# Turning the combined expert rows: TensorE transposes against a pass through HBM and VectorE's block transpose, in a fused attention and mixture-of-experts kernel

## What is computed

```python
x = hidden_states                       # (2, 1024, 512)
xn = layernorm(x)
# attention, one head of width 512, no mask
q, k, v = split(xn @ w_qkv.T + b_qkv)
s = softmax(q @ k.T / sqrt(512)) @ v @ w_out.T + b_out
# experts
logits = xn @ router_w + router_b
w = softmax(top2(logits))               # two weights for each token
h_e = silu(xn @ expert_w[e] + expert_b[e])
combined = sum over the two chosen e of w_e * h_e
y = xn + combined @ proj_w + proj_b
g = silu(norm_w * y / rms(y))
out = x + s * g
```

## Time and profile before

| | us |
|---|---|
| median of 3 runs | 490.43 (489.11 to 491.26) |
| the profiled execution | 490.71 |
| its span, first to last instruction | 489.0 |
| TensorE busy | 478.2 (98%) |
| VectorE busy | 312.5 (64%) |
| ScalarE busy | 207.7 (42%) |
| GpSimd busy | 205.4 (42%) |

### The profile page before, as it was taken

The page is one execution under the profiler, slowest core; times in us unless marked ns, Lnnn a source line. Parts: engine busy times, 40 slices in busy tenths (PEclk is TensorE's granted clock), DMA queues, the critical chain, the costliest instruction groups (busy, mean ns, idle before and its releaser), DMA issues.

```text
span 489.0 us, 7145 instructions
## 1 busy us (share of the span) xinstructions
PE 478.2 (98%) x2146; PEld 388.1 (79%) x2147; DVE 312.5 (64%) x474; ACT 207.7 (42%) x300; POOL 205.4 (42%) x289
## 2 busy tenths in 40 slices
PE   6999999999999999999999999999999999999995
PEld 3688787888888888878888888878888878888884
DVE  2657152578632436979888888762597754857762
ACT  1265463143331154736444444322655441644550
POOL 2145210005887859703000000744568873377234
PEclk9999999999999999999999999999999999999999
DMA  8764999966888599897996666897555864445512
GB/s 309 272 238 166 379 382 369 390 207 227 294 294 304 188 334 304 252 295 205 262 282 202 195 200 184 310 305 267 158 156 170 264 192 147 138 158 170 172 47 84
DMA packets 77630, 115.77 MB, mean 237 GB/s; under 512 B 6608, under 2 KB 36320, under 8 KB 77600
## 3 DMA queue, kind: packets, MB, share of 16 engines
q1 hardware_dynamic: 63872, 77.62, 50.4%
q0 software_dynamic: 7440, 25.45, 14.7%
q10 hardware_dynamic: 6288, 12.33, 7.1%
HBM read 66.09 MB, written 49.28 MB: 236 GB/s over the span
## 4 chain that ended last, share of the span: by engine, by line
PE 92%; DVE 3%; DMA 2%; issue 2%; SPq 0%; ACT 0%; DVEq 0%
PE ab L1589 20%; PE ab L1590 20%; PE ab L1591 20%; PE sc L1589 7%; PE sc L1591 7%; PE sc L1590 7%; PE sc L1605 3%; PE tp L1595 2%; DMA xg<-rows_scratch 2%; PE tp L1639 2%; DVE y L1468 1%; PE sc L1668 1%; DMA raw_v<-in_w_qkv 1%; PE ab L1613 1%; PE sc L1671 1%
## 5 line engine op out<-in xcount | busy, mean ns | idle before, releaser
L781 POOL DMA_INDIRECT y<-y_scratch,pos x32 | 33.3, 1042 | 88.8 <-DMA y_scratch<-yt_so 74.2
L1589 PE MATMUL ab<-W,st_h 128*128 x156 | 60.8, 390 | 0.6 <-DVE st_l L1297 0.6
L1591 PE MATMUL ab<-W,st_l 128*128 x156 | 60.7, 389 | 0.0
L1590 PE MATMUL ab<-W,st_h 128*128 x156 | 60.7, 389 | 0.0
L764 POOL DMA_INDIRECT rows_scratch<-xb,pos x32 | 31.2, 974 | 51.0 <-DVEq L1285 42.8
L1589 PE MATMUL sc<-xt_h,t_h 128*128 128x512 f32 x128 | 50.1, 391 | 0.0
L1591 PE MATMUL sc<-xt_h,t_l 128*128 128x512 f32 x128 | 49.8, 389 | 0.0
L1590 PE MATMUL sc<-xt_l,t_h 128*128 128x512 f32 x128 | 49.8, 389 | 0.0
L1026 ACT CAST st_h<-tp 128x512 fp32r<-128x512 f32 x39 | 22.9, 587 | 41.1 <-PE ab L1591 39.0
L1353 DVE TENSOR_REDUCE small<-sc 128x1 f32<-128x1024 f32 x16 | 19.5, 1222 | 24.3 <-PE sc L1591 21.9
L1589 PEld LDWEIGHTS ab<-W,st_h 128*128 128x128 f32 x156 | 29.3, 188 | 7.1 <-issue 1.0
(11 more groups left out here) (270 smaller groups left out, 1197.2 us busy)
## 6 DMA issues: line engine op xcount, KB each, us to landing
rows_scratch<-xn ACTq DMA_DIRECT2D x3, 3328.0 KB, 20.2
xb<-in_expert_w POOLq DMA_DIRECT2D x6, 1024.0 KB
xn<-rows_scratch SPq DMA_DIRECT2D x48, 128.0 KB, 3.4
xg<-rows_scratch SPq DMA_DIRECT2D x44, 128.0 KB
y_scratch<-yt_own SPq DMA_DIRECT2D x20, 256.0 KB, 3.1
y_scratch<-yt_so SPq DMA_DIRECT2D x19, 256.0 KB, 2.9
p_scratch<-prob SPq DMA_DIRECT2D x9, 512.0 KB, 2.9
rows_scratch<-xs SPq DMA_DIRECT2D x16, 256.0 KB, 5.9
```

The lines of the kernel that those rows point to most:

```text
L781: pool.indirect_dma_start(y[:, q, :], None, y_d, bass.IndirectOffsetOnAxis(pos[:, GB * s + p:GB * s + p + 1], 0))\
L1589: nc.tensor.matmul(dst, lh, rh, start=start, stop=False)
L1590: nc.tensor.matmul(dst, lh, rl, start=False, stop=False)
L1591: return nc.tensor.matmul(dst, ll, rh, start=False, stop=stop)
```

## The change

The eight transposes of `turn_comb` are gone from TensorE. The combined rows now take the way of the probabilities. `add_bias` writes the expert's rows with the columns in the order (a c q), so that gathered and combined rows have that order already. `pass_combined(p)` on SP waits for `combine(p)`, stores the two tiles of `y1` in HBM (`c_scratch`, 512 KB), waits for the landing, and loads them into the place of the pair's `y2` rows with four DMAs of 128 KB. `c_turn(p)` on VectorE waits for these (`comb_in`), transposes the 32x32 blocks into `tp` in two instructions, and counts `p1_turned`. `c_split` and GpSimd's `gather_pair` now wait for `p1_turned` where they waited for TensorE's `tp_full`. The tables OUT and TURN number the uses of `p1_out` and `p1_turned`, which combined rows and probabilities now share.

Three orders change with it. On VectorE `c_turn(j+3)` stands between `weigh(j+2)` and `row_max(j+2)`. On ScalarE `exp(j+2)` stands ahead of `c_split(j+3)`. On SP `pass_combined(0)` stands in the middle of the stage's first loads, 1 and 2 stand ahead of `pass_on(0)`, and the later ones behind `pass_on`, `store_1` and `load_x1` of their turn. The semaphore `bc_done` is merged into `pre`.

```diff
+    c_d = nc.dram_tensor("c_scratch", (GB, 2, P, D), F32).ap()
+    c_v = c_d.rearrange("p t s h -> p s t h")
+    c_q = c_d.rearrange("p t (r s) (a f) -> p a s t r f", r=4, a=4)
...
+            def pass_combined(p):
+
+                q = 2 * (p % 2)
+                sp.wait_ge(c_done, 2 * p + 2)
+                sp.dma_start(c_v[p], y1[:, q:q + 2, :]).then_inc(p1_out, 16)
+                sp.wait_ge(p1_out, 16 * OUT["c", p])
+                for a in range(4):
+                    sp.dma_start(y2[32 * a:32 * (a + 1), q:q + 2, :].rearrange("p t (r f) -> p (t r) f", r=4),
+                                 c_q[p, a, :, :, :, :].rearrange("s t r f -> s (t r) f")).then_inc(comb_in, 16)
+
+            pass_combined(0)
             sp.wait_ge(ab_full, U["v", 1, GB - 1] + 1)
...
-            pool.wait_ge(tp_full, 1)
+            pool.wait_ge(p1_turned, TURN["c", 0])
             gather_pair(2)
...
             def c_split(p):
-                act.wait_ge(tp_full, p + 1)
+                act.wait_ge(p1_turned, TURN["c", p])
                 nc.scalar.copy(st_h[:, :, :, :], tp[:, :, :, :]).then_inc(tp_hi, 1)
...
-                if j + 3 < GB:
-                    c_split(j + 3)
                 if j == GB - 3:
                     p_split(GB - 2)
                 if j + 2 < GB:
                     exp(j + 2)
+                if j + 3 < GB:
+                    c_split(j + 3)
...
-                vec.tensor_tensor(yt[h], ab[:, (U["e", 0] + h) % 2, :],
-                                  bias_e[:, ds(e, 1), :].rearrange("p a n -> p (a n)"), ALU.add).then_inc(ab_read, 1)
+
+                vec.tensor_tensor(yt[h].rearrange("p (a c q) -> p c a q", a=4, q=32),
+                                  ab[:, (U["e", 0] + h) % 2, :].rearrange("p (c a q) -> p c a q", a=4, q=32),
+                                  bias_e[:, ds(e, 1), :].rearrange("p o (c a q) -> p (o c) a q", a=4, q=32),
+                                  ALU.add).then_inc(ab_read, 1)
...
+            def c_turn(p):
+                q = 2 * (p % 2)
+                dve.wait_ge(comb_in, 64 * (p + 1))
+                if p == 0:
+                    dve.wait_ge(g_lo, ROWS)
+                else:
+                    dve.wait_ge(tp_lo, TU["c", p])
+                for s in range(2):
+                    last = vec.transpose(tp[:, s, :, :].rearrange("p c (r s) -> p c r s", r=4),
+                                         y2[:, q + s, :].rearrange("p (r c q) -> p c r q", r=4, q=32))
+                last.then_inc(p1_turned, 1)
...
             combine(1)
+            c_turn(0)
             c_low(0)
...
             add_product(0, 1)
+            c_turn(1)
             c_low(1)
             combine(2)
             weigh(0)
             row_max(GB)
             add_product(1, 0)
             add_product(1, 1)
+            c_turn(2)
             c_low(2)
...
                 if j + 2 < GB:
                     weigh(j + 2)
+                if j + 3 < GB:
+                    c_turn(j + 3)
+                if j + 2 < GB:
                     row_max(GB + j + 2)
...
-            def turn_comb(p):
-                pe.wait_ge(c_done, 2 * p + 2)
-                if p == 0:
-                    pe.wait_ge(g_lo, ROWS)
-                else:
-                    pe.wait_ge(tp_lo, TU["c", p])
-                q = 2 * (p % 2)
-                transpose_tile(y1[:, q, :], 0)
-                transpose_tile(y1[:, q + 1, :], 1).then_inc(tp_full, 1)
```

More of the change, by code:

```diff
@@ L109, in gated_attention_moe @@
         TU[k] = len(TU)
+    OUT, TURN = {}, {}
+    for k in ([("c", 0), ("c", 1), ("c", 2), ("t", 0)]
+              + [u for p in range(GB - 2) for u in [("t", p + 1)] + ([("c", p + 3)] if p + 3 < GB else [])]):
+        OUT[k] = len(OUT) + 1
+    for k in ([("c", 0), ("c", 1), ("c", 2), ("t", 0)]
+              + [u for j in range(GB - 2) for u in ([("c", j + 3)] if j + 3 < GB else []) + [("t", j + 1)]]):
+        TURN[k] = len(TURN) + 1
     with ExitStack() as ctx:
@@ L278, in gated_attention_moe @@
         q_hi = sem("q_hi")
-        bc_done = sem("bc_done")
         const = sem("const")
@@ L351, in gated_attention_moe @@
         p1_in = sem("p1_in")
+        comb_in = sem("comb_in")
         p1_turned = sem("p1_turned")
@@ L678, in pass_on @@
                                  p_q[j, a, :, :, :]).then_inc(p1_in, 16)
+            pass_combined(1)
+            pass_combined(2)
             pass_on(0)
@@ L693, in _ @@
                         load_x1(p + 1)
+                if p + 3 < GB:
+                    pass_combined(p + 3)
                 if p + 4 < GB:
@@ L1615, in bias_products @@
             def bias_products():
-                pe.wait_ge(bc_done, 1)
                 for m, (high, low) in enumerate(((wk_h, wk_l), (wq_h, wq_l))):
@@ L1861, in _ @@
             pe.wait_ge(*lows_done(E))
-            turn_comb(0)
             pe.wait_ge(mw_in, 32 * KC)
@@ L1867, in _ @@
             project(0)
-            turn_comb(1)
             scores(1, 0)
             project(1)
-            turn_comb(2)
             scores(1, 1)
@@ L1880, in _ @@
                     scores(1, j + 2)
-                if j + 3 < GB:
-                    turn_comb(j + 3)
                 if j == GB - 2:
```

18 lines of the change are left out of this document (9 added, 9 removed).

## The result

The changed kernel takes **527.5 us** (median of four runs, 525.1 to 529.0), the kernel before 490.9 beside it: a ratio of 1.075, 95% interval 1.070 to 1.079. It is slower by 36.7 us where I forecast 18.3 (509.0, 498 to 522). The direction was right; the size was half of what came, and outside the range. One execution of a later run, e11_cfirst, took 967.7 us, nearly twice its five others, and is left out of its median and ratio.

A forecast was written before the change was run, and what follows sets the result against it. TensorE, busy 98% of the span and on the chain, bounds the kernel. New pauses of 25.3 us minus 7.0 for removed transposes give +18.3 on 490.7, so 509.0 us, range 498 to 522.

The forecast's parts named there:

- Round trip: 7.5 us: Last stage, between combine and c_turn: store 3.2 us plus loads 4.3 us through HBM.
- my upper bound of 9.4: Longest trip allowed for in the range: stores of 3.94 and loads of 5.5 us, giving 520.4 us.
- `combine` quicker when the gathers fall elsewhere: Part of the partly hidden rival: additions 0.7 instead of 1.2 us each, short trips, 497 us; chance 0.05.
- the loop from one `c_low` to the next: Last stage's turns: VectorE's chain through the round trip takes 19.4 us against TensorE's 16.35, a pause of 3.1 each turn.
- The clock was a rival: Last stage: TensorE's clock falls to 1.2 GHz for a block after three pauses, 5.45 us each, about 525; chance 0.07.
- GpSimd's gathers wait for `c_turn` of two pairs earlier, a turn before they are needed: Last stage, GpSimd: the gathers' new wait was listed under edits that cost nothing.
- the transposes at -7.0: Last stage, TensorE: removing eight turn_comb of 0.88 us each from the chain saves 7.0 us.
- `add_bias` at nothing: Expert stage, VectorE: the new column order costs 0, bounds 0 and 0.41 us; a wait of 0.24 per tile covers it.
- the start's 5.3: Start of the last stage, third key_weights group: TensorE pauses 5.3 us, or 3.3 if rows are back before 326.9.
- the loads at 4.3: Round trip's second part, four loads in the last stage: 4.3 us, between 3.7 from below and 8.0 from above.
- What fails is the order of its waits, not its load: VectorE in the last stage has room, 13.6 of 16.35 us busy per turn; its in-order waits make the loss.
- rows in time: Rival: rows always return in time, trips under 5.7 us with SP free; 487.0 us, down to 483.7; chance 0.11.

The follow-up runs named there:

- e11_cfirst: e10_sp with c_turn(j+3) ahead of row_max(j+2) on VectorE and c_split ahead of exp on ScalarE: 500.6 us, ratio 1.022.
- e12_gather: The changed kernel with GpSimd's gather(j+4) moved behind inverse_rms(j+2), away from the store of the combined rows: 524.9 us, ratio 1.071.
- e6_start: The changed kernel with row_max ahead of c_turn, combine(j+4) ahead of attn_fin(j), pass_combined a turn earlier and the stage's start reordered: 512.5 us, ratio 1.042.
- e4_rowmax: The changed kernel with row_max(j+2) ahead of c_turn(j+3) on VectorE, nothing else: 518.8 us, ratio 1.055.
- e1_fill: The changed kernel with matmuls of no use filling TensorE's pauses in the last stage: 530.9 us, ratio 1.080.
- e7_sp: The changed kernel with pair 1's store and loads right behind pair 0's on SP, ahead of the ten loads: 527.3 us, ratio 1.072.
- e3_nowait: The changed kernel with c_turn reading combine's sum in y1 without waiting for rows from HBM; the next gathers wait for the loads: 499.9 us, ratio 1.017.
- e2_bias: The kernel before with only the changed kernel's bias addition (four runs of 32 in place of one of 512): ratio 1.001.
- e9_wide: The changed kernel with c_scratch laid out so the store writes 4 KB in a row per partition, not two pieces of 2 KB: 533.4 us, ratio 1.088.
- e13: The changed kernel with the edits of e4_rowmax and e12_gather together: 517.9 us, ratio 1.055.
- e8_nowait2: e3_nowait with pair 1's store and loads moved ahead of the large loads on SP: 496.8 us, ratio 1.011.
- e10_sp: e6_start with both stores issued before one wait on SP, combine(3) ahead of c_turn(2), gate rows in three loads: 500.6 us, ratio 1.022.

## Why the prediction was wrong, step by step

The last column is the time from one `project` to the next (in the first row, up to `project(0)`) against the kernel before. Its forecast is the forecast pause less 0.88 for the transposes.

| place | pause forecast | measured | trip beyond 7.5 | longer, start to start (forecast) |
|---|---|---|---|---|
| start | 5.3 | 6.05 | (rows 1.0 later) | 6.9 (4.4) |
| `project(1)` | 0 | 2.2 | store 13.7 | 1.5 (-0.9) |
| `project(2)` | 1.6 | 1.3 | 1.5 | 2.3 (0.7) |
| `project(3)` | 7.6 | 11.0 | 3.6 | 10.4 (6.7) |
| `project(4)` | 3.1 | 3.3 | 3.0 | 5.5 (2.2) |
| `key_weights(1, 1, n)` | 1.5 | 0 | | 0.3 (0.6), up to `project(5)` |
| `project(6)` | 3.1 | 7.2 | 4.0 | 6.5 (2.2) |
| `project(7)` | 3.1 | 1.3 | 0.7 | 3.3 (2.2) |
| sum | 25.3 | 32.35 | | 36.7 (18.3) |

**The step that failed is a term of the sum: "Round trip: 7.5 us".** The trips took 8.2 to 11.5, 10.0 in the mean of pairs 2 to 4, 6 and 7, and 18.5 for pair 1. Even my upper bound of 9.4 lies below that mean. I had the store from the rows of the probabilities and took 3.2 "since the new stores too stand among other transfers". They do, but among others. The old stores are issued behind `exp`, most of them in a quiet moment. The new ones are issued behind `combine`, when SP has just issued the transfers of its turn and GpSimd is at its gathers. The trace before had it, in GpSimd's timeline of the turn of the earlier trace rows, which I did not show and did not price:

```profile
422.91 1.67 POOL L808 TENSOR_TENSOR so<-so,x 128x512 f32<-128x512 f32 x1 [9.63 <-DVE so L1522]
424.73 1.27 POOL L781 DMA_INDIRECT y<-y_scratch,pos  x1
```

`combine` ends there at 425.13, so a store behind it meets the gathers that start at 424.73. The same two rows correct what I read off `combine`. I wrote of "two additions that run beside GpSimd's gathers" and of 1.2 us for each in place of 0.7. In fact the first takes 0.75 and the second 1.78, and what runs beside the second is GpSimd's own addition of 128x512 elements (`add_x1`); `combine(2)`, beside gathers alone, takes 0.74 and 0.75 in the same trace. The 2.4 us of the sum stay, the reason was wrong, and so was the rival's "`combine` quicker when the gathers fall elsewhere": in e12_gather they do and the second addition still takes 1.78. With the gathers elsewhere and nothing else changed the store took 3.6 to 5.5 (e12_gather, pairs 3 to 7), and by itself, in e6_start, 2.8. The Trainium skill's fit for GpSimd's path (DMA: Bandwidth & Descriptors, "Anatomy of one DMA") gave 3.2 for the store as my rows did: 0.4 above what a store by itself took here, and it says nothing of what stands beside it.

**With that term most of the working holds.** With the measured trips (13.8 us more in the six places of the table) the forecast's own sum is 25.3 + 13.8 - 7.0 = 32.1, or 522.8 us. Of the 4.7 that are still missing 3.9 arise up to `project(1)`, where pair 1 was stuck (below). Place by place: 7.6 + 3.6 = 11.2 against 11.0 ahead of `project(3)`; the loop from one `c_low` to the next 19.4 + 3.0 = 22.4 against 418.89 - 396.17 = 22.7; 3.1 + 4.0 = 7.1 against 7.2 ahead of `project(6)`. The longest pause is ahead of `project(3)`, SP's order made it, and e4_rowmax took `row_max` and `exp` out of the loop for 8.7 us, where 10 were expected by the loop.

**The clock was a rival, and is no cause of the loss.** I gave it 0.07 and 525 us, and that the time landed near there is luck: it added 16 us of slow blocks to pauses of 25. The clock fell in the pauses as it said, and the Trainium skill's sentence that an idle array falls back (TensorE: Matmul & The Clock Gate, "What's actually happening") agrees with the windows here: 0.56 and 0.55 behind pauses of 11.0 and 7.2. But the price is another: 9.8 us of slower matmuls and, by e1_fill, no time that filling the array brings back, since each slow stretch of the changed kernel but 0.15 us behind `project(7)` stands ahead of a later wait. (Behind the last pause of e1_fill, with no wait to come, 1.5 us of them did cost.) That is also why `key_weights(1, 1, n)` shows no pause where I forecast 1.5: the slow block ahead of it hid it, and in e1_fill, at full clock, it is 1.4. And it is why two pauses look forecast well: ahead of `project(4)` the loop was 3.3 longer than I said and the block before it 2.9 longer, and ahead of `project(7)` it was 0.7 longer and the block 2.7. Whoever adds the pauses and the slow matmuls gets the total; whoever takes either for a cause by itself errs.

**What was missed outright.** `project(1)`: `pass_combined(1)` stands behind the ten loads at the stage's start. I costed the loads that stand ahead of pair 0, and not these ten ahead of pair 1 in the same queue. It costs a pause of 2.2 and, by e7_sp, 3.2 us at the start of `project(2)`, but only 0.2 in the median time. "GpSimd's gathers wait for `c_turn` of two pairs earlier, a turn before they are needed" was right for the turns and wrong at the start, where `gather(3)` waited 12.4 us; in e3_nowait that wait alone was worth a pause of 8.3.

**Right.** The direction, for which the Trainium skill's rule to transpose 128x128 on TensorE (VectorE: DVE Perf Modes, "Rules for kernel authors") spoke too, and 490.9 against 527.5 us agrees; the transposes at -7.0; `add_bias` at nothing (e2_bias); the start's 5.3, nearly (6.05, with the rows back at 329.9 in place of 328.9; 6.8 to 7.6 in the executions of e4, e9, e12 and e13, where the start is the same); the loads at 4.3 (4.3 to 4.8 in five of seven trips). "What fails is the order of its waits, not its load": VectorE is busy 62% of the span. The rival "rows in time", 487.0, was wrong by more than its condition: in e8_nowait2, where TensorE, ScalarE and VectorE wait for no row and only GpSimd's gathers do, the time is 496.8.

What stays open: those 496.8, and the 500.6 of e10_sp, are made of pauses of 1 to 4 us that I have named but not taken away one by one. I haven't separated in e9_wide whether the load's pattern alone made it slower, nor how much of a slow store is due to the transfers ahead of it in its own queue.

## What to carry to other kernels

Take the price of a transfer from rows where it has the same neighbours, and not only the same bytes and queue: before you cost a new store, read which transfers its own queue and other engines issue in that very window. When a queue waits in line for a landing, everything behind it has the trip in front of it, so issue what is ready first and wait afterwards. And don't add a slower clock behind a pause to the pause: if the next block waits for a loop that doesn't pass through TensorE, the slow matmuls only fill it, and only behind the last pause do they cost; put useless matmuls there and look.

## What the runs showed of the hardware

- A store of 512 KB from SP's queue landed in 2.75 to 2.82 us with next to nothing beside it (five stores in e6_start), in 3.6 to 5.5 just behind other transfers of its own queue (pairs 3 to 7 of e12_gather), in 4.6 to 6.8 with GpSimd's four gathers issued at about the same time, most of them with such transfers too (pairs 2 to 6 of the changed kernel), and in 13.7 behind ten loads of 4 MB. The size of the pieces, 2 or 4 KB, made no difference.
- The first matmuls behind a pause of 2.19 us were at the lower clock (0.79 us for the first), those behind one of 3.32 at first were not (0.51), though some us later they were (0.72 over 418 to 424). The length of the pause alone did not say it. Behind pauses of 7 and 11 us the low stretch lasted some 6 us.
- VectorE's additions and products of two 128x512 operands from SBUF can stretch while GpSimd adds tiles of the same size, and not while it only issues gathers: the second addition of `combine` took 1.78 us beside `add_x1` and 0.75 beside gathers alone (355.01, pair 2), and once `times_s`, beside two additions of GpSimd, 3.73 in place of 0.68. Not every one that overlaps does: the first addition of `combine` stays at 0.75 with 0.5 us of `add_x1` beside it.

```profile
405.47 3.73 DVE L1550 TENSOR_TENSOR yy<-yy,s 128x512 f32<-128x512 f32 x1
```
